# Maximum matmuls, turns and P·V as entries of the order tables, with new tables for the loop

## The reference

```python
x = x + attn(layernorm(x))                  # scores[0,-1] and scores[-1,0] are set to -1e9
x = x + cross_attn(layernorm(x), ctx)       # softmax over 64 context rows, times tanh(gate)
x = x + ffn(layernorm(x))                   # a = entmax15(layernorm(x @ proj))
# ffn: h = gelu(((x,1) @ Win1 * (a @ C1)) @ Wout1.T);  out = ((h,1) @ Win2 * (a @ C2)) @ Wout2.T
```

## Time and profile before

| | |
|---|---|
| median of 3 runs | 1161.67 us (1156.67 to 1162.15) |
| the profiled execution | 1160.25 us, of which the span is 1158.4 us |
| PE busy (matmuls) | 1042.9 us, 90% |
| DVE busy | 768.1 us, 66% |
| ACT busy | 625.3 us, 54% |
| granted TensorE clock, mean | 0.935 of full |
| the chain that ended last | PE 57%, DVE 18%, ACT 11%, issue 9% |

### The profile page before, as it was taken

How to read it: one execution, slowest core, us unless ns; L and a number is a source line. 1 busy time by engine, 2 the same in 40 slices (tenths; PEclk the granted TensorE clock), 3 DMA queues, 4 the chain that set the end, 5 groups by cost and what they waited for, 6 DMA issues and landing times.

```text
span 1158.4 us, 16341 instructions
## 1 busy us (share of the span) xinstructions
PE 1042.9 (90%) x5310; PEld 598.8 (52%) x5310; DVE 768.1 (66%) x1575; ACT 625.3 (54%) x850; POOL 150.2 (13%) x174
## 2 busy tenths in 40 slices
PE   5898989889888999799989998999989997997977
PEld 4544333446444655465545654565546554655754
DVE  3574554677777867886687768786788577715762
ACT  2345655534554666465647474757556654664522
POOL 2000000012002210221011200220022102201311
PEclk9899988979996999999988999899989997998988
DMA  5677674721240142112411041104111310030001
GB/s 151 168 207 223 196 225 120 225 67 26 74 146 11 28 137 66 47 28 61 142 46 28 18 164 46 34 12 159 49 39 28 132 52 20 10 119 19 1 1 37
DMA packets 91288, 97.41 MB, mean 84 GB/s; under 512 B 10547, under 2 KB 76790, under 8 KB 89174
## 3 DMA queue, kind: packets, MB, share of 16 engines
q1 hardware_dynamic: 91222, 96.63, 28.2%
HBM read 41.34 MB, written 29.36 MB: 61 GB/s over the span
## 4 chain that ended last, share of the span: by engine, by line
PE 57%; DVE 18%; ACT 11%; issue 9%; DMA 3%; SPq 1%; POOL 1%; DVEq 0%; ACTq 0%
PE y_ps L758 17%; PE x_ps L758 13%; PE st_ps L758 9%; PE pv_ps L758 7%; PE sm_ps L758 5%; ACT probs L1190 3%; ACT L1190 3%; DVE mx L1390 2%; DVE cst L1480 2%; DVE cst L1473 2%; PE y_ps L905 2%; PE y_ps L872 1%; DMA xa<-in_x 1%; DMA a_scr<-a_cat 1%; ACT xt_hi L1190 1%
## 5 line engine op out<-in xcount | busy, mean ns | idle before, releaser
L1390 DVE TENSOR_REDUCE mx<-sm_ps 128x2 f32<-128x1024 f32 x256 | 312.7, 1222 | 170.2 <-PE sm_ps L758 161.5
L1190 ACT ACTIVATE probs<-st_ps 128x1024 f32<-128x1024 f32 x256 | 261.9, 1023 | 197.1 <-PE st_ps L758 196.0
L758 PE MATMUL st_ps<-q_st,k_st 52*128 52x512 f32 x512 | 206.9, 475 | 15.2 <-ACT probs L1190 13.5
L758 PE MATMUL sm_ps<-k_st,q_st 50*128 50x512 f32 x512 | 182.2, 478 | 6.6 <-DVE nm L1404 4.0
L758 PE MATMUL pv_ps<-probs,v_all 128*32 128x512 f32 x1024 | 148.3, 654 | 0.0
L758 PEld LDWEIGHTS st_ps<-q_st,k_st 52*128 52x128 f32 x512 | 84.2, 194 | 118.7 <-issue 68.5
L758 PE MATMUL x_ps<-b_cat,pt 128*128 128x256 f32 x448 | 114.7, 387 | 0.0
L758 PEld LDWEIGHTS x_ps<-b_cat,pt 128*128 128x128 f32 x448 | 78.4, 190 | 30.1 <-issue 18.4
L522 POOL TENSOR_TENSOR px<-px,cst 128x512 f32<-128x512 f32 x56 | 58.1, 1043 | 216.2 <-DVE cst L1485 216.1
L1190 ACT ACT_TABLE_LOAD x64 | 82.1, 1283 | 5.1 <-PE y_ps L758 3.2
L758 PEld LDWEIGHTS sm_ps<-k_st,q_st 50*128 50x128 f32 x512 | 70.7, 194 | 24.3 <-DVE mx L1390 12.1
(11 more groups left out here) (299 smaller groups left out, 1766.0 us busy)
## 6 DMA issues: line engine op xcount, KB each, us to landing
a_scr<-a_cat SPq DMA_DIRECT2D x32, 512.0 KB, 4.8
a_cat<-a_scr SPq DMA_DIRECT2D x8, 2048.0 KB, 8.1
q_st<-qk_hi SPq DMA_DIRECT2D x128, 64.0 KB, 2.3
k_st<-qk_hi SPq DMA_DIRECT2D x128, 64.0 KB, 2.3
b_scr<-b_cat SPq DMA_DIRECT2D x8, 1024.0 KB, 6.5
b_cat<-b_scr SPq DMA_DIRECT2D x8, 1024.0 KB, 9.7
xa<-in_x SPq DMA_DIRECT2D x9, 512.0 KB, 3.6
q_st<-qk_lo SPq DMA_DIRECT2D x64, 64.0 KB, 2.3
```

Of the source, the lines that this page charges most:

```text
L758: return nc.tensor.matmul(dst, lhs, rhs, start=start, stop=stop, **kw)
L1190: return nc.scalar.activation(dst, src, f, **kw)
L1390: nc.vector.tensor_reduce(mx[:, c % 2, :].rearrange("p (m x) -> p m x", m=2)[:, :, col], sm_ps[:], axis=AX, op=ALU.max).then_inc(sm_taken, 1)
```

## The change

The score pair keeps its place at each even tick. The maximum pair (`M`), the turn (`TN`) and P·V (`PV`) become entries of the tables, on PE and on DVE; a function `emit` on each engine carries an entry out. The three tables of the loop are drawn up anew: nearly every entry stands at another place. Passes 2 to 6 use them. For passes 0, 1 and 7 and for the tail the old order is written out as tables of its own (`EARLY_*`, `LAST_*`, `TAIL_*`); there each alternating group of four matmuls becomes a score pair followed by a maximum pair, and the rest of PE's order of pass 7 and the tail is as it was.

```diff
-    (0, "V", 0, 0), (0, "V", 0, 1), (0, "V", 1, 0), (0, "V", 1, 1), (1, "X1", 0, 0), (2, "OT", 0, 0), (2, "X1", 1, 0),
+    (0, "PV", 15, 0), (0, "M", 0, 0), (0, "V", 0, 0), (0, "V", 0, 1), (0, "V", 1, 0), (0, "V", 1, 1), (0, "X1", 0, 0),
...
+            def score_pair(b, t):
+                for r in (t % 4, t % 4 + 1):
+                    scores(b, t // 16, t // 4 % 4, r)
+
+            def max_pair(b, j):
+
+                c, i, r0 = j // 8, j // 2 % 4, 2 * (j % 2)
+                for r in (r0, r0 + 1):
+                    if c < 2:
+                        for_max(b, c + 2, i, r)
+                    else:
+                        for_max(b + 1, c - 2, i, r)
...
+            def emit(b, kind, i, part):
+
+                if kind == "P":
+                    score_pair(b, i)
+                elif kind == "M":
+                    max_pair(b, i)
+                elif kind == "TN":
+                    turn_max(*((b, i + 1) if i < CH - 1 else (b + 1, 0)))
+                elif kind == "PV":
...
-            def iteration(b, project=True, setup_from=None):
-                for t in range(0, TICKS, 2):
...
+            def iteration(b):
+                for t in range(TICKS):
+                    if t % 2 == 0:
+                        score_pair(b, t)
+                    for tick, kind, i, part in PE_TASKS:
+                        if tick == t:
+                            emit(b, kind, i, part)
...
-            iteration(first, setup_from=SETUP_TICKS)
-            iteration(At(None, 1), setup_from=SECOND_TICKS)
+            for b, kind, i, part in EARLY_PE:
...
-            iteration(At(None, B - 1), project=False)
-            for go, kind, i, part in TAIL_PE:
-                task(At(None, go), kind, i, part)
+            for b, kind, i, part in LAST_PE:
+                emit(At(None, b), kind, i, part)
+            for b, kind, i, part in TAIL_PE:
+                emit(At(None, b), kind, i, part)
```

More of the change, by code:

```diff
@@ L422, in order @@
             return SETUP_UNITS + before + len(PLAN) * (g.off - 2) + n
-        early = []
-        for t in range(SECOND_TICKS + TICKS):
-            early += [u[1:3] for u in plan(At(None, 0)) if u[0] == t - SECOND_TICKS]
-            early += [u[1:3] for u in SETUP_PE if u[0] == t]
+        early = [(u[0], u[2]) if u[1] == "SW" else u[1:3] for u in EARLY_PE if u[1] not in X_BANK and u[3] == 0]
         def setup_no(p, n):
@@ L510, in ln_passed @@
             count = 0
[L511 to L512 removed]
+            for u in LAST_DVE + TAIL_DVE:
+                if u[0] == LAST + 1 and u[1] in (f"LN{n + 1}S", f"LN{n + 1}M"):
                     count += 1 if u[1][-1] == "S" else 2
[L514 removed]
+                if u == (LAST + 1, kind, i):
                     return 8 * LAST + count
@@ L977, in down @@
                 if k == 0:
-                    pe.wait_ge(o_taken, At(None, LAST).times(4, 0) if in_tail(g) else g.times(4, 4))
+                    pe.wait_ge(o_taken, At(None, LAST).times(4, 0) if g.reg is None and g.off >= LAST else g.times(4, 4))
                     wait(pe, z2_taken, g.times(1, -1))
@@ L1167, in _ @@
             pe.wait_ge(rows_in, 16 * 12)
-            for t in range(0, SETUP_TICKS, 2):
-                for r in (t % 4, t % 4 + 1):
-                    for_max(first, t // 16, t // 4 % 4, r)
-                setup(t)
-                if t == 16:
-                    turn_max(first, 0)
-                setup(t + 1)
-            iteration(first, setup_from=SETUP_TICKS)
-            iteration(At(None, 1), setup_from=SECOND_TICKS)
+            for b, kind, i, part in EARLY_PE:
+                if kind == "SW" and b < 0:
+                    setup_ctx(i)
+                elif kind == "SW":
+                    setup_unit(b, i)
+                else:
+                    emit(At(None, b), kind, i, part)
             iteration(At(None, 2))
@@ L1330, in iteration @@
                         softmax_exp(b, t)
-                    dense(b + -1, t, project, not is_first(b), scores=True)
-                    if setup_from is not None:
-                        setup(setup_from + t)
-                if not project:
-                    save_chunk(b, CH - 1)
+                    for tick, kind, i in ACT_TASKS:
+                        if tick == t:
+                            emit(b, kind, i)
             def w_hi_part(n):
@@ L1362, in _ @@
             act.wait_ge(tanh_done, 1)
-            for t in range(SETUP_TICKS):
-                setup(t)
-            iteration(At(None, 0), setup_from=SETUP_TICKS)
-            iteration(At(None, 1), setup_from=SECOND_TICKS)
+            for b, kind, i in EARLY_ACT:
+                if kind == "SW":
+                    setup_unit(b, i)
+                else:
+                    emit(At(None, b), kind, i)
             iteration(At(None, 2))
@@ L1759, in _ @@
             dve.wait_ge(const_ready, CONSTS)
-            for t in range(0, SETUP_TICKS, 2):
-                reduce_max(first, t // 16, t // 4 % 4, t % 4)
-                setup(t)
-                if t == 16:
-                    negate_max(first, 0)
-                setup(t + 1)
-                if t == 14:
-                    for k in range(TT):
-                        ln_apply(0, xa, xa, second, k)
-            iteration(first, setup_from=SETUP_TICKS)
-            iteration(At(None, 1), setup_from=SECOND_TICKS)
+            for b, kind, i in EARLY_DVE:
+                if kind == "SW":
+                    setup_unit(b, i)
+                else:
+                    emit(At(None, b), kind, i)
             iteration(At(None, 2))
```

234 lines of the change are left out of this document (93 added, 141 removed), and 331 rows, old and new, of tables (ACT_TASKS, DVE_TASKS, EARLY_ACT, EARLY_DVE).

## The result

| | before | after |
|---|---|---|
| median | 1161.91 us (4 runs) | 1123.9 us (4 runs, 1120.83 to 1125.84) |
| span of the profiled execution | 1158.4 | 1119.0 |
| PE busy | 1042.9, 90% | 1014.4, 91% |
| DVE busy | 768.1, 66% | 764.1, 68% |
| ACT busy | 625.3, 54% | 623.4, 56% |

The ratio is 0.9692, 95% interval 0.965 to 0.9734: 3.1% faster, where 12 us of 1160, 1.0%, were forecast.

What follows compares the result with a forecast made beforehand. PE was taken to set the pace (115.55 of 123.60 us busy), often waiting for DVE. Terms for waits, clock, lone pairs, X2 and held-back pairs summed to -2.4 us a pass, five times: 1160.25 - 12 = 1148 us, range 1130 to 1170.

Steps and rivals of the forecast that it cites:

- much faster: Rival, chance 0.14: the clock no longer falls and X2 is covered, -6.3 us a pass, 1129 us.
- The clock: Behind the ON stretch: half of 10.2 us at the lower level goes, at 0.22 each; -1.1 us a pass, bounds 0 and -2.2.
- held-back pairs: Inside groups: score and maximum pairs no longer wait behind each other; -0.8 us a pass, bounds 0 and -1.2.
- the 0.43 and 0.67: Sign of being right: on PE, lone pairs cost 0.43 us and groups 0.67 us.
- Waits taken away: PE waits from OT to the output projection: 3.96 us go, less 0.5 for latencies; -3.5 us a pass, bounds -1.5 to -5.0.
- X2 to S: Between X2 and S: less PE work covers the way through ACT and DVE; +1.3 us a pass, range 0 to 2.
- Between maximum pairs 16 and 17: In the loop: many units on PE and DVE there, T waits for C; +0.3 us a pass, range 0 to 1.
- Pairs that stand alone: Maximum pairs outside groups in the loop: 18 alone and 23 groups, with form changes; +1.4 us a pass, range 1.2 to 2.3.
- At nothing: No cost or gain from loop restart, ACT table loads, SP and POOL; no term for passes outside the loop.
- Slower by the exponential of tick 34: Rival, chance 0.18: PE waits for ACT's exponential at P·V 8, 3 to 4 us once a pass; 1168 us.
- Same: Rival, chance 0.22: waits of the first stretch move instead of going; 1157 to 1164 us, say 1160.
- The order in a group at 0.86: Rival, chance 0.04: score, score, maximum, maximum makes a group cost 0.86 us instead of 0.67; 1185 us.

Runs made afterwards that it cites:

- e1: The kernel before with its order kept in every pass, only each group's matmuls as score, score, maximum, maximum; 1147.65 us.
- e2: The changed kernel with the four matmuls of each group alternating again, as in the kernel before, everywhere; 1146.4 us.
- e4: The changed kernel with the first output projection directly behind the turn in passes 2 to 6; 1164.99 us.
- e11: e4 with unused matmuls in its two waits: six ahead of the output projection, eight ahead of the first G; 1151.02 us.
- e5: The changed kernel with two lone score pairs of the loop (ticks 14 and 20) placed beside a maximum pair, on PE alone; 1131.48 us.
- e3: The changed kernel with the new loop order only up to tick 21 on all engines and the old order behind it; 1150.58 us.
- e9: e1 with unused matmuls in passes 2 to 6: eight ahead of the output projection, four ahead of X2; 1163.28 us.
- e15: e1 with only DVE's list changed: entmax pieces 2 to 6 early, the next image's statistics late; 1171.28 us.
- e14: The changed kernel with entmax pieces 4, 5 and 6 back behind ON on DVE; 1160.83 us.
- e7: The changed kernel with the new loop order only up to tick 28 (through H 2), the old order behind it; 1138.16 us.

## Why the prediction was wrong

**Direction right, size wrong by a factor of three**: 38 us in place of 12. The time lies 6 us below the range and 5 below the rival that I called much faster. Three steps of the sum failed. The clock was mis-sized at -1.1 a pass: 8.5 us a pass at the lower level went and not 5, and by the prices below that is about -2.8. The held-back pairs were put at -0.8, and the runs give -1.5 (e1) to -2.9 (e2). The passes outside the loop were put at nothing, and the two traces differ by 7.5 us there. Of the signs that I had set, the output projection's wait, the 0.43 and 0.67 and the wait of S came as written; only the pass shrank by 6 us and not by 2 to 3. By its steps, per pass, from the means of passes 3 to 6 (before 123.1 us, PE busy 115.0; after 116.9, busy 111.2):

- *Waits taken away, -3.5.* 3.96 to 0.40: -3.56. Right. *X2 to S, +1.3.* 0.27 to 1.48: +1.21. Right. *Between maximum pairs 16 and 17, +0.3*: no wait. All idle time fell by 2.4 us a pass (8.1 to 5.7); the terms for waits sum to -1.9.
- *Clock, -1.1.* This is the term that was mis-sized. The time at the lower level fell from 9.4 us a pass to 0.9, not to half. And each microsecond of it costs more than the 0.22 that I had from the two intervals of the earlier trace rows: by the passes before, from 121.1 us with 3.4 us at the lower level to 124.3 with 13.7, it is 0.31; in the changed kernel 1.8 us for 3.4 (118.20 against a mean of 116.4 without, though these scatter by 1.5 us among themselves); between e4 and e11 3.1 us for 7.7, 0.40. At 0.33, my choice near the low end of these, the term is -2.8. PE's busy time says the same from another side: it fell by 3.8 us a pass, but between passes with the same 3.4 us at the lower level only from 112.72 to 112.36, so nearly all of the 3.8 went with the lower clock. The bounds of 0 and -2.2 did not hold it, since I had set "half" by judgement and bounded with the too low price.
- *Held-back pairs, -0.8.* -1.5 by e1, part of which may be the clock, and -2.9 by e2 under the new tables. The step failed in what it looked at: I counted the open waits inside groups and not that half of each pair holds the other chain back, so that a reduction starts 0.3 to 0.4 us late without an idle row on PE.
- *Pairs that stand alone, +1.4.* The prices stand: a pair alone 0.43 (PE goes on from 579.31 at 579.74), a group 0.67. e5 put two pairs back and gained nothing, so the sum of these prices is no gain that is to be had by moving them. No run measures the +1.4 as a whole; the trace has 24 groups and 16 pairs alone in a pass, since a group spans the seam of two passes, and by the same prices that is +1.5 in place of +1.7.
- *At nothing* for the passes outside the loop: the spans differ by 7.5 us there. Pass 7 took 114.2, 118.0 and 115.6 us in the three traces with alternating groups there and 108.9 to 114.5 in the thirteen with the same order as two and two, about 3 us less on average. The rest is passes 0 and 1, whose sum ranges over 228.2 to 238.3 us between kernels with the very same order there. Everything outside the loop takes 529.7 to 543.9 us in thirteen traces with this order and 540.9 to 542.3 in the three with alternating groups, so how much of the 7.5 belongs to the change is not settled. What moves them is open.

The four sizes for a pass, -2.4 (idle time), -2.8, +1.4 and -1.5 to -2.9, give -5.3 to -6.7; measured are 6.2 (passes 3 to 6). That they meet is no proof: they overlap, since a held pair is sometimes idle time too, and the price of the clock and the +1.4 are not exact. What doesn't overlap is busy and open time of PE: 3.8 and 2.4.

**The rivals.** Slower by the exponential of tick 34: no idle row there. Same: the waits of the first stretch did go. The order in a group at 0.86: not so, 0.67. Much faster, 1129 us: its condition (the clock no longer falls) came true; its other one (X2 covered) did not, and the group order made up for that and more.

**The cause, as far as it is settled.** I explained the 2.09 us and the clock behind it by one late result and took its removal for the gain. The runs show that removing it is not worth much by itself: e3 removed it and gained nothing, and in e9, where it was filled, 0.8 us of it was left eight microseconds later. e15 moved DVE's pieces alone and lost 24 us. In the old order PE went behind ON by what DVE delivered; the waits on PE were where this came out. Of the 38 us, 22 are lost when the group order alone is put back (e2) and 24 when the tables alone are (e1); each is worth more with the other. The tables gave their part only where three things stood together: DVE's entmax pieces out of that stretch (without: e14, nothing left), cover for PE until DVE's chain lets X2 start (without: e3), and the second half drawn to match (without: e7, 15 us less in the loop). Why the last half gives 14.8 us in the loop is shown only as the 2.0 us of waits a pass that it removes behind the seam of e7. Why the group order is worth more under the new tables is open.

## What to carry to other kernels

With in-order engines, price a new order as a whole: a wait that is taken away at one place returns at the next place that the late engine feeds, unless that has cover too, and one unit out of place can cost several times its own wait. When one instruction group feeds two engines, let each engine's part be complete before the other's begins; the group's own price does not show this, the starting times of its readers do. Before counting on an idle row, ask which engine paces the stretch: if filling the row with dead work makes the next row grow, PE was not what held the stretch up. And look where the filling itself stands afterwards: dead work that meets no wait any more is a cost of its own, as in e9.

## What was not expected of the hardware

- The lower of the two levels of TensorE's clock (1.2 of 2.4 GHz) followed idle stretches of PE and was kept away for the most part by work that nothing uses: e11 against e4, 0.97 to 1.00 in place of 0.93 to 0.99, 14 us by the medians. In e9 the same means moved the fall from 31 to 42 us into the pass (e1, passes 3 to 6) to 39 to 41 us and did not prevent it.
- What a microsecond at the lower level costs depended on the place: 0.22 to 0.31 in the order before, 0.40 between e4 and e11. The 0.5 of one pass of the changed kernel is within the scatter of its passes.
- Pass 0, in one and the same order on all engines, took 115.9 to 122.2 us in the profiles of fourteen kernels: 6 us that belong to no edit here. A difference of a few us outside the loop can't be read from one trace.
